# An adaLN block in float32 on one core: the shared expert's tiles all before the routed slots, whose rows are added into the output by DMA

## The reference

```python
h = _layernorm(x) * (1 + ca) + sa
x = x + ga * attn(h)          # gated cumulative mix, then a SwiGLU with DFF = 2048
h = _layernorm(x) * (1 + cb) + sb
logits = h @ gate_w           # E = 8 experts
top_logits, top_idx = top_k(logits, 2); top_gates = softmax(top_logits)
out_e = gelu(h @ w1[e] + b1[e]) @ w2[e] + b2[e]            # inner width H = 256
routed = sum over the two chosen e of gate * out_e
shared = gelu(h @ shared_w1 + shared_b1) @ shared_w2 + shared_b2    # inner width 512
x = x + gb * (routed + shared)
```

## Time and profile before

| | us |
|---|---|
| three runs, median (lowest, highest) | 2305.76 (2301.07, 2306.4) |
| profiled execution, its time | 2310.44 |
| profiled execution, its span | 2308.6 |
| busy in the span: PE, DVE, ACT, POOL | 1981.0, 1366.0, 690.0, 688.1 |
| mean granted clock of PE | 0.932 |

### The profile page before, as it was taken

How to read it: one execution, slowest core, us unless ns; L and a number is a source line. 1 busy time by engine, 2 the same in 40 slices (tenths; PEclk the granted TensorE clock), 3 DMA queues, 4 the chain that set the end, 5 groups by cost and what they waited for, 6 DMA issues and landing times.

```text
span 2308.6 us, 23801 instructions
## 1 busy us (share of the span) xinstructions
PE 1981.0 (86%) x8424; PEld 1533.7 (66%) x8424; DVE 1366.0 (59%) x2190; ACT 690.0 (30%) x1168; POOL 688.1 (30%) x442
## 2 busy tenths in 40 slices
PE   7877777865999999999999999999884199998865
PEld 3655555644888888887878777787653177776653
DVE  4799999978554555566445554457764044444534
ACT  3555555532111112111122122211321044444211
POOL 4765666563000000034001110113462322222553
PEclk9988888977999999999999999999987599999987
DMA  6000001032111111123022212212552254544785
GB/s 241 19 37 37 37 37 50 21 112 92 55 55 55 46 37 37 55 96 134 19 92 64 86 51 98 93 57 74 173 188 56 64 156 129 133 132 163 185 253 144
DMA packets 87234, 211.31 MB, mean 92 GB/s; under 512 B 20282, under 2 KB 20538, under 8 KB 80046
## 3 DMA queue, kind: packets, MB, share of 16 engines
q1 hardware_dynamic: 67614, 154.39, 18.8%
q0 software_dynamic: 19504, 55.39, 9.7%
HBM read 136.91 MB, written 73.43 MB: 91 GB/s over the span
## 4 chain that ended last, share of the span: by engine, by line
PE 58%; DVE 25%; issue 7%; ACT 3%; DMA 3%; POOL 3%; SPq 1%; DVEq 0%; POOLq 0%; ACTq 0%
PE bank L729 10%; PE bank L730 10%; PE bank L731 10%; PE bank L734 5%; PE bank L736 5%; PE bank L735 5%; PE bank L1005 3%; DVE kv_t L1457 3%; DVE wc_t L1459 3%; DVE x_t L1438 2%; POOL w_post L720 2%; DMA w_post<-routed_rows,place_t 1%; DVE rs_x L1404 1%; PE bank L1007 1%; PE bank L1028 1%
## 5 line engine op out<-in xcount | busy, mean ns | idle before, releaser
L729 PE MATMUL bank<-x_hi,w_blk 128*128 128x512 f32 x1408 | 588.3, 418 | 66.8 <-DVE s_t L1540 25.1
L730 PE MATMUL bank<-x_lo,w_blk 128*128 128x512 f32 x1408 | 562.0, 399 | 0.0
L731 PE MATMUL bank<-x_hi,w_blk 128*128 128x512 f32 x1408 | 561.2, 399 | 0.0
L729 PEld LDWEIGHTS bank<-x_hi,w_blk 128*128 128x128 f32 x1408 | 274.1, 195 | 149.1 <-issue 47.3
L730 PEld LDWEIGHTS bank<-x_lo,w_blk 128*128 128x128 f32 x1408 | 274.0, 195 | 65.6 <-issue 11.1
L731 PEld LDWEIGHTS bank<-x_hi,w_blk 128*128 128x128 f32 x1408 | 272.6, 194 | 59.7
L1540 DVE TENSOR_TENSOR s_t<-act_t,bank 128x512 f32<-128x512 f32 x128 | 87.8, 686 | 298.1 <-PE bank L731 291.3
L1206 ACT ACTIVATE s_hi<-s_t 128x512 fp32r<-128x512 f32 x128 | 80.9, 632 | 486.5 <-DVE s_t L1540 472.5
L644 POOL DMA_INDIRECT slot_list<-pay,pos x64 | 64.0, 1000 | 526.7 <-DVE pos L1677 509.6
L734 PE MATMUL bank<-w_blk,s_hi 128*128 128x512 f32 x512 | 200.6, 392 | 0.0
L736 PE MATMUL bank<-w_blk,s_lo 128*128 128x512 f32 x512 | 199.4, 389 | 0.0
(11 more groups left out here) (267 smaller groups left out, 3470.6 us busy)
## 6 DMA issues: line engine op xcount, KB each, us to landing
x_t<-y_scratch SPq DMA_DIRECT2D x19, 1024.0 KB, 4.8
residual<-r_t SPq DMA_DIRECT2D x19, 1024.0 KB, 4.3
routed_rows<-o_t SPq DMA_DIRECT2D x71, 256.0 KB
r_t<-residual SPq DMA_DIRECT2D x11, 1024.0 KB
raw<-w_swi POOLq DMA_DIRECT2D x12, 768.0 KB, 4.5
x_a<-x SPq DMA_DIRECT2D x8, 1024.0 KB, 4.8
y_scratch<-kv_t SPq DMA_DIRECT2D x8, 1024.0 KB, 3.8
r_t<-x_tok SPq DMA_DIRECT2D x8, 1024.0 KB
```

What stands on the lines that cost most here:

```text
L729: nc.tensor.matmul(dst, w[:, 0, col:col + P], rhs_hi, start=start, stop=False)
L730: nc.tensor.matmul(dst, w[:, 0, col:col + P], rhs_lo, start=False, stop=False)
L731: return nc.tensor.matmul(dst, w[:, 1, col:col + P], rhs_hi, start=False, stop=stop)
```

## The change

All eight shared tiles now run before the slots, on the same buffers (`x_t`, `x_hi`, `x_lo`, `r_t`), and each tile is stored to `out` instead of `x1_dram`. SP loads the lists in four groups of 18, 18, 18 and 17, after the store of tiles 3, 4, 5 and 6. b1r is loaded after the store of tile 7 has landed. Experts 6 and 7 take the place of the shared weights in SBUF, so their pieces R0+12 to R0+15 wait for the last tile's products.

A slot's output is scaled by the gate on ACT into `p_t`, then multiplied by the row of gb on DVE. That row is made for each slot from a mask of the slot's tokens of the second sequence (`late_t`), since a slot can hold tokens of both. POOL then adds the 128 rows into `out` by token number, with one indirect DMA (`scatter`), which waits until the one before has landed. Unused places of a list point to 128 further rows of `out`. Rows are gathered six slots ahead. `places()`, `o_dram`, the indirect reads, `end(i)` and the tail are gone; ACT and DVE start the first slot after the last store to `out` has landed.

```diff
-    E_PLACE = (32, 48, 64, 80, 0, 16, 140, 156)
+    E_PLACE = (32, 48, 64, 80, 0, 16, 96, 112)
...
-        rows_t = [at(f"rows_t{i}", 194 + 2 * i, [P, D]) for i in range(3)]
+        rows_t = [at(f"rows_t{i}", 140 + 2 * i, [P, D]) for i in range(6)]
+        NR = len(rows_t)
+        p_t = [at(f"p_t{i}", 164 + 2 * i, [P, D]) for i in range(2)]
+        gb_row = at("gb_row", 168, [P, D])
+        o_t = [at(f"o_t{i}", 176 + 2 * i, [P, D]) for i in range(4)]
...
-        GROUPS = (0, 4, 16, NSLOT)
+        GROUPS = (0, 18, 36, 54, NSLOT)
...
-            for t in range(PRE):
+            for t in range(NT):
                 if t == 0:
                     gates_out(LAST - 1)
                     hT_out(LAST)
-                if t + 1 < PRE:
+                if t + 1 < NT:
                     gates_in(t + 1)
-                if t + 2 < PRE:
+                if t + 2 < NT:
                     next_x("s", t + 2)
-                if t == PRE - 1:
+                if t == 2:
                     gates_out(LAST)
+                    sp.wait_ge(b2_ok, 1)
+                    load_gain(1)
+                sp.wait_ge(ffn["s"].ev_ok, NSUB * (t + 1))
+                sp.dma_start(tokens(out, t), r_t[:, :, :]).then_inc(out_st, 16)
+                sp.wait_ge(out_st, 16 * (t + 1))
+                if t < LAST:
+                    load_r(x1_dram, t + 1)
+                if 3 <= t < LAST:
+                    if t == 3:
+                        sp.wait_ge(lst_st, 16 * 2 * NSUB * NT)
+                        sp.wait_ge(n2.tab_ok, 1)
+                    for j in range(GROUPS[t - 3], GROUPS[t - 2]):
                         row = sp.value_load(tab[0:1, 0, j:j + 1], min_val=0, max_val=LIST_ROWS - P)
-                        sp.dma_start(lst[:, j, :], list_dram[bass.ds(row, P), :]).then_inc(ls_in[group_of(j)], 16)
-                        if j == GROUPS[1]:
-                            sp.wait_ge(ffn["s"].dn, NB_S * PRE)
-                            sp.dma_start(b1r_t[:, :], b1r).then_inc(b1r_in, 16)
...
+                        sp.dma_start(lst[:, j, :], list_dram[bass.ds(row, P), :]).then_inc(ls_in[t - 3], 16)
+            sp.wait_ge(ffn["s"].dn, NB_S * NT)
+            sp.dma_start(b1r_t[:, :], b1r).then_inc(b1r_in, 16)
...
+            def scatter(j):
+                pool.wait_ge(rt.o_ok, j + 1)
+                if j == 0:
+                    pool.wait_ge(out_st, 16 * NT)
+                if j >= 1:
+                    pool.wait_ge(sc_st[(j - 1) % 2], 16 * ((j - 1) // 2 + 1))
+                pool.indirect_dma_start(
+                    out, bass.IndirectOffsetOnAxis(ap=lst[:, j, 0:1], axis=0), o_t[j % 4][:, :], None,
+                    compute_op=ALU.add).then_inc(sc_st[j % 2], 16)
+            pool.wait_ge(n2.tab_ok, 1)
+            pool.wait_ge(g_st, 16 * NT)
+            for i in range(R0 + 10, R0 + 12):
                 split_piece(i)
+                fetch(i + 2)
+            pool.wait_ge(ffn["s"].up, NB_S * NT)
...
+            for j in range(3):
                 gather(j)
+            for j in range(4):
+                pool.wait_ge(ffn["s"].dn, NB_S * LAST + 2 + 2 * (j // 2))
+                split_piece(R0 + 12 + j)
+                if j < 2:
+                    fetch(R0 + 14 + j)
+            for j in range(3, NR):
+                gather(j)
+            for j in range(NSLOT):
+                scatter(j)
+                if j + NR < NSLOT:
+                    gather(j + NR)
...
             def slot_o(j):
                 act.wait_ge(rt.dn, j + 1)
+                if j == 0:
+                    act.wait_ge(out_st, 16 * NT)
                 if j >= 2:
-                    act.wait_ge(o_st[j % 2], 16 * (j // 2))
-                nc.scalar.activation(o_t[j % 2][:, :], bank_o[j % 2][:, :], ACT.Copy,
+                    act.wait_ge(rt.o_ok, j - 1)
+                nc.scalar.activation(p_t[j % 2][:, :], bank_o[j % 2][:, :], ACT.Copy,
                                      scale=lst[:, j, 1:2].bitcast(F32)).then_inc(rt.og_ok, 1)
...
+            def slot_o(j):
+                if j >= 1:
+                    dve.wait_ge(rt.o_ok, j)
+                nc.vector.scalar_tensor_tensor(out=gb_row[:, :], in0=gbd_t[:, :], scalar=late_t[:, j:j + 1],
+                                               in1=gbs_t[0][:, :], op0=ALU.mult, op1=ALU.add).then_inc(rt.gr_ok, 1)
+                dve.wait_ge(rt.gr_ok, j + 1)
+                dve.wait_ge(rt.og_ok, j + 1)
+                if j >= 4:
+                    dve.wait_ge(sc_st[j % 2], 16 * ((j - 4) // 2 + 1))
+                nc.vector.tensor_tensor(o_t[j % 4][:, :], p_t[j % 2][:, :], gb_row[:, :],
+                                        ALU.mult).then_inc(rt.o_ok, 1)
+            dve.wait_ge(out_st, 16 * NT)
+            for k in range(4):
+                dve.wait_ge(ls_in[k], 16 * (GROUPS[k + 1] - GROUPS[k]))
+            then(nc.vector.tensor_scalar(late_t[:, :], lst[:, :, 0], float(T_SEQ * TT), None, ALU.is_ge))
             slot_x(0)
             e_now = expert(0)
+            dve.wait_ge(b1r_in, 16)
             slot_u(0, e_now)
             slot_x(1)
             for j in range(NSLOT):
                 if j + 2 < NSLOT:
                     slot_x(j + 2)
                 slot_g(j)
+                if j >= 1:
+                    slot_o(j - 1)
                 if j + 1 < NSLOT:
                     e_next = expert(j + 1)
                     slot_u(j + 1, e_next)
                     e_now = e_next
+            slot_o(NSLOT - 1)
...
-    out = nc.dram_tensor("out", (n, D), F32, kind="ExternalOutput").ap()
+    out = nc.dram_tensor("out", (n + P, D), F32, kind="ExternalOutput").ap()
```

More of the change, by code:

```diff
@@ L241, in build @@
         b1r_in, b2_in, tb_in, gs_in = sem("b1r_in"), sem("b2_in"), sem("tb_in"), sem("gs_in")
[L242 to L252, removed]
+        b2_ok, g_st = sem("b2_ok"), sem("g_st")
+        gi_in, gin_ok, late_ok = sem("gi_in"), sem("gin_ok"), sem("late_ok")
+        ls_in = [sem(f"ls_in{i}") for i in range(4)]
+        rw_in = [sem(f"rw_in{i}") for i in range(6)]
+        sc_st = [sem("sc_st0"), sem("sc_st1")]
+        rt = sems("routed", "tr_ok xh_ok xl_ok up u1_ok u_ok gl_ok gt_ok gh_ok gl_lo dn og_ok gr_ok o_ok")
         PASS = {"a": 0, "b": 1, "c": 2, "s": 3}
@@ L293, in build @@
         SP_PIECES = 8
-        GROUPS = (0, 4, 16, NSLOT)
+        GROUPS = (0, 18, 36, 54, NSLOT)
         def group_of(j):
[L298 to L305, removed]
+            return sum(j >= first for first in GROUPS[1:-1])
         def norm_bank(u):
@@ L1054, in _ @@
                 e_now = e_next
-            pe.wait_ge(rt.og_ok, NSLOT)
-            for t in range(PRE, NT):
-                shared_tile(t)
         @block.scalar
@@ L1276, in take_gin @@
                     act.wait_ge(ffn["s"].dn, NB_S * (t - 1))
-                nc.scalar.activation(gin_of(t)[:, :], graw[t >= PRE][:, :], ACT.Copy).then_inc(gin_ok, 1)
+                nc.scalar.activation(gin[t % 2][:, :], graw[:, :], ACT.Copy).then_inc(gin_ok, 1)
             def split_s(t):
                 act.wait_ge(ffn["s"].up, NB_S * t)
-                split(x_in, 16 * (2 * NT + t + 1), 1.0, None, False, *x_of("s", t)[0:2])
-            for t in range(PRE):
+                split(x_in, 16 * (2 * NT + t + 1))
+            for t in range(NT):
                 for s in range(NB_S):
@@ L1348, in _ @@
             slot_o(NSLOT - 1)
-            act.wait_ge(rt.dn, NSLOT)
-            for t in range(PRE, NT):
-                split_s(t)
-                for s in range(NB_S):
-                    block_s(t, s)
-                    if s == 2:
-                        take_gin(t)
         @block.vector
@@ L1804, in evacuate_s @@
                     dve.wait_ge(gs_in, 16 * (t // T_SEQ + 1))
-                    fix_gain(gbs_t, tmp[0])
+                    fix_gain(gbs_t[t // T_SEQ], tmp[0])
+                    if t > 0:
+                        then(nc.vector.tensor_tensor(gbd_t[:, :], gbs_t[1][:, :], gbs_t[0][:, :], ALU.subtract))
                 dve.wait_ge(f.dn, NB_S * (t + 1))
                 dve.wait_ge(r_in, 16 * (2 * NT + t + 1))
-                gain_and_add(f, t, gbs_t)
-            for t in range(PRE):
+                gain_and_add(f, t, gbs_t[t // T_SEQ])
+            for t in range(NT):
                 for s in range(NB_S):
@@ L1949 @@
     b2p = np.concatenate([b2, b2, np.zeros((32 - 2 * E, D), np.float32), b2])
-    first = [32 * KB // 4 + e * 4096 for e in range(4)] + [0, 4096] + [140 * KB // 4, 156 * KB // 4]
+    first = [32 * KB // 4 + e * 4096 for e in range(4)] + [0, 4096] + [96 * KB // 4, 112 * KB // 4]
     steps = np.zeros((2, E), np.float32)
```

194 lines of the change are left out of this document (33 added, 161 removed).

## The result

The changed kernel takes 2325.7 us (median of 4 runs, 2323.7 to 2330.1), the kernel before 2303.5 us beside it (4 runs, 2301.1 to 2306.4). The ratio is 1.0098, with a 95% interval of 1.0077 to 1.012: it is slower by 1%, where I forecast 1.3% faster. The profiled execution has a span of 2323.8 us; my sum was 2276.5 us. So 47.3 us are to be found.

What follows compares the result with a forecast made beforehand. It took queue-made idle before the slots, PE's work in them, and a tail as bounds. First scatter at 1899.5, plus 376 for 71 serial additions, plus about 1, gave 2276.5 us span, 2274 at the median; range 2222 to 2360.

Steps and rivals of the forecast that it cites:

- the passage: From the last tile's end to the first scatter: residual, store landing, b1r load, first output; 1869.5 to 1899.5 us.
- rival 2: POOL's wait ahead of each scatter: an addition's landing exceeds 5.75 us, so slower than before; 71 us per microsecond; chance 0.29.
- The serial additions: Slots: each scatter waits for the last one's landing; round trip 3.73 + 0.6 + 1.0 = 5.3 us, 71 times, 376 us.
- What is queued behind the wait: POOL's queue: a gather behind each scatter, needed six slots later, costs only issue time inside the landing.
- The engines: Slots: two more DVE operations of 0.69 us; the engines alone would run at 4.25 instead of 4.02 us a slot.
- rival 4: Slots: PE's clock falls because PE waits; at half clock 71 x 6.8 gives 2381 us; chance 0.04.
- Rival 3: POOL held up writing descriptors while DVE uses SBUF operands; 5 us more in every slot gives over 2600 us; chance 0.04.
- The list loads in tiles 3 to 6: SP's queue: eighteen loads make a round of 26.0 against 24.3 us; PE doesn't notice, tile 7's store leaves 5.2 us late.
- The gain: Removed: the 93 us hole before the slots (PE busy 18.7) and the 193 us tail, of which 121.7 return as tiles.

Runs made afterwards that it cites:

- 10.8 us of the late start taken back: Changed kernel with eight of the 18 list loads between a tile's store and the wait for its landing, in tiles 3 to 6: 2312.4 us, 1.0033 of before.
- the pace mended alone: Changed kernel with each scatter cut into left and right 256 columns, each waiting only for the same half of the slot before: 2284.4 us, 0.9916 of before.
- the halves: The scatters of 256 columns (128 KB) in the changed kernel with scatters cut in two: 2284.4 us; with eight list loads also inside the store's wait, 2271.9 us.
- the run without the binding wait: Changed kernel with odd slots added into a second DRAM buffer, each scatter waiting for the last but one, output incomplete: 2235.1 us, 0.971 of before.
- the best complete form of the change: Changed kernel with both edits, eight list loads inside the wait for the store's landing and scatters in two halves: 2271.9 us, 0.9864 of before.

## Why the prediction was wrong

*The direction.* The prediction named the point at which it turns, a round trip of 5.75 us with the passage as forecast, and rival 2 as what would bring it. With the passage at 1915.7 us the point moves to (2308.6 - 1 - 1915.7) / 71 = 5.52 us. The round trip came out at 5.74, within 0.1 of the old point, and that alone would have made no difference that can be measured; the passage alone, at 5.3 us a round, would have left a gain. It took both misses to make the kernel slower. The runs agree: with 10.8 us of the late start taken back it is 1.0033 of before, with the pace mended alone 0.9916.

*The serial additions: the term that was mis-sized.* The sum was 3.73 (lone gather) + 0.6 (issue) + 1.0 (transfer) = 5.3. The runs give 2.7 (plain scatter) + 0.6 + 1.5 = 4.8 to 4.9 until landing, and 0.8 until the next start. The issue term was right. The base was 1.0 too long, the transfer 0.5 too short, and POOL's turnaround of 0.8 was missing from the sum: 3.73 us is the time to PE's go, not to POOL's next DMA. So 5.3 lies near 5.74 in part by luck, since the first of these errors hides most of the other two. The transfer I had worked out as a difference (2.0 us at 132 GB/s less 1.0 us of a plain one); the rate was right, as the halves show.

*What is queued behind the wait* was right: the gather stood inside the landing and cost nothing there. *The engines* at 4.25 us: 4.43 in the run without the binding wait. Hidden as predicted, so it cost nothing. The clock in the slots was 0.92, which rival 4 had feared at 0.50; since POOL stood for the landing ahead of 65 of the 71 scatters, a slower PE does not show in the pace. Rival 3 did not come in its size of 5 us; in small (0.3 us in the mean, 0.5 at most) it is in the issues that start inside `o_t`.

*The list loads in tiles 3 to 6: the step that failed.* SP's round of 26.0 us took the median landing of a store, 4.5 us; the maximum of 10.8 stood in the same row. The first round held (26.3), but the stores of tiles 4 and 5 went out right behind a 1 MB load, landed in 8.6 and 8.7 us, and made rounds of 30.7 and 30.0. That the loads have 10 us or more in hand, so that PE doesn't notice, counted x and x1 and not the gate rows, which were 12.3 us late for ACT. Without the 8.5 us of the two long landings the gate rows would have gone out at 1857.5 and landed by about 1861.7. PE had work until 1867.7, so it would not have noticed (an estimate from these rows). The step's cover was there for four tiles and gone in the last; moving eight loads into the wait brought back 13 us.

*The passage.* The last tile ended at 1884.0 instead of 1869.5 us, and it took 31.7 instead of 30.0 us from there. The 1.7 hide a residual of 8.9 us instead of 5.2, because moved work (POOL's pieces) now lies beside it, and slower landings, against the lag of SP that had already been paid ahead of the last tile.

*The gain* was right in size (hole and tail are gone), but two thirds of the hole were no gain of the order of tiles and slots. I read from the earlier trace rows that SP's queue made it, and did not ask what else than this change would remove it.

## What to carry to other kernels

A serial chain of DMAs is priced from start to landing plus the turnaround of the engine that waits, and each part has to come from a row of its own. Where one is in flight, the first question is whether two can be (another target, halves of a row), and the second what the issue then costs. When small loads are put into a busy queue, list everything behind them down to the smallest, and take the landing of a neighbour beside the transfer that runs with it. And a hole that comes from a queue's order can be closed in that queue: here 2255 us by that, against 2272 by the best complete form of the change.

## What the runs showed of the hardware that I had not expected

- An indirect scatter of 128 rows of 2 KB into DRAM lands in 2.7 us, an adding one in 4.8 to 4.9, of which 1.6 instead of 1.0 us is issue on POOL. Adding ones of 1 KB rows land in 3.8 us with the same issue.
- POOL starts its next DMA 0.3 us after the last one's issue if the wait is met, and 0.8 us after the landing if it is not.
- The landing of a tile's 1 MB store took 8.6 and 8.7 us where a 1 MB load went out 0.4 us ahead of it. In the six other places of the same run it took 4.4 (twice), 5.8, 6.3, 6.6 and 10.9 us, the last 2.6 us behind such a load.
- An adding scatter's issue took 1.56 us where DVE worked on neither `o_t` nor `gb_row`, and 1.8 to 1.9 us in the mean where it started inside `o_t`.
- After 6.98 us of idling PE worked off the rest of a tile at a clock of 0.50.
